# Deferring the evacuation of the energy matmuls behind the next tile's normalization, and a self-wait on every DMA transpose

## The chip, the cores and the metric

The kernel runs on one Trainium2 chip with 8 cores, each running the same program on its own data with no exchange between them. The metric is the device time of the slowest core in microseconds (us); lower is better. PE is the matmul engine (TensorE), DVE the vector engine, ACT the scalar engine, POOL GpSimd, SP the sync engine, which here only issues DMAs.

## The reference, cut to what matters

Input x is 4 batches of 4096 tokens of 1024 numbers. One layer is an attention block and a feed-forward block, each fed by a layernorm and each followed by a layernorm and a residual add.

```python
xn = layernorm(x)                              # stage A
s  = xn @ W_spin.T + b_spin                    # stage A
g  = mean(s, over tokens) @ W_global.T         # stage B
e  = s @ W_J.T                                 # stage A, "energy"
local = softmax(e @ s.T / 32) @ s              # stage C
x1 = x + layernorm(tanh(beta * (s + g + local)))        # stage 2
h  = silu(xn2 @ Wg.T) * (xn2 @ Wu.T)           # stage 3, xn2 = layernorm(x1)
out = x1 + layernorm(h @ Wd.T)                 # stage 4
```

A core takes one half (2048 tokens) of one batch as its own. It needs s for all 4096 tokens of the batch, but e, the attention output and the feed-forward block only for its own 2048.

## The kernel before, in words

The program is written engine by engine with explicit semaphores. Each helper emits its instructions at the end of the queue of the engine that it names, and each engine runs its queue strictly in the order of emission. So the order in which the Python code calls the helpers is the order of work, and an instruction that waits holds back everything behind it on its engine.

**Stage A** walks over 32 tiles of 128 tokens, numbered k. A tile passes through these steps, all of them with two buffers by the parity of k:

- `emit_xchunk(c)`, line 168, SP: loads tiles 2c and 2c+1 of x (1 MB). The load of a chunk waits for `pa_apply` of the odd tile that frees its buffer, and is issued at once after it.
- `pa_stats(k)`, lines 186 to 197: mean and variance on DVE, then the square root on ACT.
- `pa_apply(k)`, lines 210 and 215, DVE: the normalized tile `xn_bf`.
- `pa_xntr(k)`, line 232, a DMA transpose issued from ACT: `xn_bf` into `xnT_sb`.
- `pa_mm(k)`, lines 252 and 256, PE: twice a bias matmul and 8 matmuls of 128x512, into `ps_s`.
- `pa_bias(k)`, line 267, ACT: copies `ps_s` to `s_tok`.
- `pa_stra(k)`, line 277, a DMA transpose issued from ACT: `s_tok` into `s_FM`.

Between these lie the 32 **energy groups**, numbered gi, which exist for the first 16 tiles only. Group gi is 8 matmuls on PE into one of two halves of `ps_e` (line 306), an evacuation on DVE to `e_stage` (line 318), and a write of 128 KB to DRAM issued from POOL (line 327). Eight groups (one `tb`) need four transposed tiles of `s_FM`. The matmuls of group gi wait for the evacuation of group gi-2, and the evacuation of gi waits for the DRAM write of gi-2.

The loop over k emits, in this order: statistics of tile k, normalization and transpose of tile k-1, copy and transpose of s of tile k-2, matmuls of tile k-1, and then as many energy groups as are allowed: the four tiles of s must have been emitted, and gi must be below 2(k-3). A group becomes possible only every fourth k, and so 4, 2, 2 and 0 groups are emitted in turn from k = 5 to k = 20.

The DVE queue between two tiles is thus: statistics of k, normalization of k-1, evacuations of the groups that PE computes after tile k-1, then statistics of k+1, normalization of k, and so on.

**Stage B** (lines 381 to 460) forms the mean and g. **Stage C** takes 16 tiles of 128 queries against 4096 keys in four quarters: scores on PE (line 526), their maximum on DVE (545, 549), the exponential on ACT (570), a DMA transpose issued from ACT (589), a correction by DVE (646), and the second matmul on PE (678). The exponential of a quarter waits for the transpose of the same quarter of the query tile before (line 567), because both use one quarter of `P_sb`. **Stage 2** (lines 803 to 892) forms x1 and its normalized, transposed copy without PE. **Stage 3** (984, 995, 1018) and **stage 4** (1088) are the feed-forward block.

The DMA transposes increment one of four semaphores: `dtp[0]`, `dtp[1]`, `dts[0]`, `dts[1]`. In stage A each takes every second tile; in stage C each belongs to one quarter; in stage 2 `dtp` takes every second tile.

Of the kernel before, what the change touches and what calls it, by code (L numbers as in the profile page):

```python
# [20 lines left out]
KC = D // P  # L21
# [14 lines left out]
def build_program():  # L36
# [19 lines left out]
    with ctx:  # L56
# [20 lines left out]
        def vinc(sem, instr, k=1):  # L77
            instr.then_inc(sem.h, k)
            sem.n += k
            return sem.n  # L80
# [13 lines left out]
        rec = {}  # L94
        sdefer = []

        def s_add(fn):
            sdefer.append(fn)

        def s_flush():  # L100
            fns = list(sdefer)
            del sdefer[:]
            if fns:
                def run(s, fns=fns):
                    for f in fns:
                        f(s)
                block.scalar(run)
# [68 lines left out]
        def pa_stats(k):  # L176
            c, par = k // 2, k % 2
            xsl = xs[:, c % 2, par, :]
            w_sq = rec.get(("sqrt", k - 2), 0)

            def fvA(v, k=k, c=c, par=par, xsl=xsl, w_sq=w_sq):
                w = rec[("xchunk", c)]
                v.wait_ge(w[0].h, w[1])
                if w_sq:
                    v.wait_ge(ss.h, w_sq)
                v.bn_stats(out=st6[:, par, 0:6], in_=xsl[:, 0:512])
                i = v.bn_stats(out=st6[:, par, 6:12], in_=xsl[:, 512:1024])
                vinc(sv, i)
                v.wait_ge(sv.h, sv.n)
                i = v.bn_aggr(out=mvb[:, par, :], in_=st6[:, par, :])  # L190
                vinc(sv, i)
            block.vector(fvA)
            rec[("statsA", k)] = sv.n

            def fsq(s, k=k, par=par, wA=sv.n):
                s.wait_ge(sv.h, wA)
                s.activation(out=sqv[:, par, :], in_=mvb[:, par, 1:2],
                             func=AF.Sqrt, bias=eps_col[:]).then_inc(ss.h, 1)
            s_add(fsq)
            ss.n += 1  # L200
            rec[("sqrt", k)] = ss.n
# [62 lines left out]
        def pa_bias(k):  # L264
            def fsb(s, k=k, par=k % 2, wt=rec[("mm", k)]):
                s.wait_ge(st.h, wt)
                s.copy(out=s_tok[:, k, :], in_=ps_s[:, par, :]).then_inc(ss.h, 1)
            s_add(fsb)
            ss.n += 1
            rec[("biasS", k)] = ss.n  # L270

        def pa_stra(k):
            sem = dts[k % 2]

            def fdt(s, k=k, sem=sem):
                s.wait_ge(ss.h, rec[("biasS", k)])
                s.dma_start_transpose(
                    out=s_FM[:, :, k * P:(k + 1) * P],
                    in_=s_tok[:, k, :]).then_inc(sem.h, 16)
            s_add(fdt)  # L280
            sem.n += 16
            rec[("stra", k)] = (sem, sem.n)
            if k % 4 == 3:
                rec[("stra4", k // 4)] = (dts[0].n, dts[1].n)

        e_sc_w = e_d.rearrange("n p j t -> p n j t")
        eq_groups = [(m, tb) for tb in range(4) for m in range(KC)]
        eg_state = {"i": 0}

        def emit_energy_group():  # L290
            gi = eg_state["i"]
            m, tb = eq_groups[gi]
            eg_state["i"] = gi + 1
            slot = gi % 2
            w_wr = rec.get(("e_wr", gi - 2), 0)

            def fte(t, m=m, tb=tb, slot=slot, gi=gi):
                if gi == 0:
                    t.wait_ge(dwB.h, 16)
                w4 = rec[("stra4", tb)]  # L300
                t.wait_ge(dts[0].h, w4[0])
                t.wait_ge(dts[1].h, w4[1])
                if gi >= 2:
                    t.wait_ge(sv.h, rec[("e_evac", gi - 2)])
                for j in range(KC):
                    i = t.matmul(ps_e[:, slot, :],  # L306
                                 wjT_sb[:, j, m * P:(m + 1) * P],
                                 s_FM[:, j, tb * 512:(tb + 1) * 512],
                                 start=(j == 0), stop=(j == KC - 1))
                vinc(st, i)  # L310
            block.tensor(fte)
            rec[("e_mm", gi)] = st.n

            def fve(v, m=m, tb=tb, slot=slot, gi=gi, w_wr=w_wr):
                v.wait_ge(st.h, rec[("e_mm", gi)])
                if w_wr:
                    v.wait_ge(w_wr[0].h, w_wr[1])
                i = v.tensor_copy(out=e_stage[:, slot, :], in_=ps_e[:, slot, :])  # L318
                vinc(sv, i)
            block.vector(fve)  # L320
            rec[("e_evac", gi)] = sv.n

            sem = deG[gi % 2]

            def fgw(gp, m=m, tb=tb, slot=slot, gi=gi, sem=sem):
                gp.wait_ge(sv.h, rec[("e_evac", gi)])
                gp.dma_start(
                    out=e_sc_w[:, 4 * tb:4 * tb + 4, m, :],
                    in_=e_stage[:, slot, :].rearrange("p (a t) -> p a t", a=4)
                    ).then_inc(sem.h, 16)  # L330
            block.gpsimd(fgw)
            sem.n += 16
            rec[("e_wr", gi)] = (sem, sem.n)
            if (m, tb) == (KC - 1, tb):
                rec[("e_tb", tb)] = (deG[0].n, deG[1].n)

        for k in range(NT_ALL + 2):
            if k < NT_ALL:
                pa_stats(k)
            if 1 <= k < NT_ALL + 1:  # L340
                pa_apply(k - 1)
                pa_xntr(k - 1)
            if 2 <= k:
                pa_bias(k - 2)
                pa_stra(k - 2)
            if 1 <= k < NT_ALL + 1:
                pa_mm(k - 1)
                if (k - 1) % 2 == 1:
                    c2 = (k - 1) // 2 + 2
                    if c2 < NT_ALL // 2:  # L350
                        emit_xchunk(c2)
            while (eg_state["i"] < len(eq_groups)
                   and ("stra", 4 * eq_groups[eg_state["i"]][1] + 3) in rec
                   and eg_state["i"] < max(0, (k - 3)) * 2):
                emit_energy_group()
        while eg_state["i"] < len(eq_groups):
            emit_energy_group()
        s_flush()
        ctxA1.close()
        sv_pa_done = rec[("apply", NT_ALL - 1)]  # L360
# [218 lines left out]
        def c_fptr(qt, qi):  # L579
            par = qt % 2  # L580
            sem = ptx[qi]
            w_pv = rec.get(("pvb", qt - 2, qi), 0)

            def fptr(s, qt=qt, qi=qi, par=par, sem=sem, w_pv=w_pv,
                     wss=rec[("expq", qt, qi)]):
                s.wait_ge(ss.h, wss)
                if w_pv:
                    s.wait_ge(st.h, w_pv)
                s.dma_start_transpose(  # L589
                    out=PT_sb[:, par, qi * 1024:(qi + 1) * 1024]  # L590
                    .rearrange("p (j q) -> p j q", j=8),
                    in_=P_sb[:, qi * 1024:(qi + 1) * 1024]
                    ).then_inc(sem.h, 16)
            s_add(fptr)
            sem.n += 16
            rec[("ptr", qt, qi)] = (sem, sem.n)
# [8 lines left out]
        for qt in range(NT_OWN):  # L605
            par = qt % 2
# [262 lines left out]
        def l2_grpB(t_i):  # L869
            par = t_i % 2  # L870

            def fv2b(v, t_i=t_i, par=par):
                v.wait_ge(ss.h, rec[("sq3", t_i)])
                i = v.reciprocal(out=rsig2[:, par, :], in_=sqv2[:, par, :])
                vinc(sv, i)
                v.wait_ge(sv.h, sv.n)
                if t_i >= 2:
                    w = rec[("xtr", t_i - 2)]
                    v.wait_ge(w[0].h, w[1])
                i = v.tensor_scalar(out=xn2_bf[:, par, :], in0=x1_buf[:, par, :],  # L880
                                    scalar1=mvb2[:, par, 0:1],
                                    scalar2=rsig2[:, par, :],
                                    op0=ALU.subtract, op1=ALU.mult)
                vinc(sv, i)
            block.vector(fv2b)
            rec[("xn2", t_i)] = sv.n

            sem_tr = dtp[t_i % 2]

            def fs3b(s, t_i=t_i, par=par, sem=sem_tr, wv=rec[("xn2", t_i)]):  # L890
                s.wait_ge(sv.h, wv)
                s.dma_start_transpose(
                    out=xn2T[:, :, t_i * P:(t_i + 1) * P],
                    in_=xn2_bf[:, par, :]).then_inc(sem.h, 16)
            s_add(fs3b)
            sem_tr.n += 16
            rec[("xtr", t_i)] = (sem_tr, sem_tr.n)
# [71 lines left out]
        for hb in range(HC):  # L969
            par = hb % 2  # L970
# [106 lines left out]
        for t_i in range(NT_OWN):  # L1077
            par = t_i % 2
# [140 lines left out]
```

## Time and profile before

| | us |
|---|---|
| median of 3 runs (lowest, highest) | 1571.98 (1570.0, 1573.46) |
| profiled execution, its own time | 1574.13 |
| its span on the slowest core, core 7 | 1572.6 |
| spans of the eight cores | 1557.6 to 1572.6 |
| PE busy over the span | 1208.0 (77%) |
| DVE busy | 495.0 (31%) |
| ACT busy | 223.1 (14%) |
| mean DMA rate over the span | 83 GB/s |

All times below are of the profiled execution, on core 7, counted from the start of its span. "Idle before" is the time in which an engine had nothing running ahead of an instruction, with what ended it.

### The profile page before, as it was taken

The page shows a single profiled execution, that of the slowest core. Times are in us where ns is not written, and L with a number is a line of the kernel's source. Part 1 is how long each engine was busy: PE and PEld are TensorE (multiplying, and loading weights), DVE is VectorE, ACT ScalarE, POOL GpSimd, SP SyncE. Part 2 cuts the span into 40 slices and gives each one's busy share as a digit, 9 for nine tenths or more (in the row PEclk, how much of TensorE's full clock was granted, in tenths as well). Part 3 has the DMA queues.
Part 4 walks back from the last instruction along what each step waited for, and adds up shares of the span by engine and source line. Part 5 has one row for each costly group of instructions (what it writes and reads, how often), then busy time and mean ns, then how long its engine had stood idle before and what let it go on. Part 6 is the DMA issues. An engine that isn't in the chain of part 4 may idle for free.

```text
span 1572.6 us, 14760 instructions; the slowest of 8 cores (1557.6 to 1572.6 us)
## 1 busy us (share of the span) xinstructions
PE 1208.0 (77%) x5274; PEld 517.5 (33%) x5274; DVE 495.0 (31%) x860; ACT 223.1 (14%) x359; POOL 72.9 (5%) x92
## 2 busy tenths in 40 slices
PE   0746556568699899989998970009999999999997
PEld 0212122122234344434443430004444444444443
DVE  2221222232124333433343335751222111124334
ACT  0100000011022211211122111001111111110000
POOL 0000011000000000000000000010111111100000
PEclk9977688689889999989999995559999999999999
DMA  9533333285422321222123117976453645503332
GB/s 189 101 91 81 74 80 74 67 189 113 71 50 47 68 48 41 63 52 47 41 50 65 41 27 230 292 141 78 40 71 37 76 46 57 64 28 107 108 107 80
DMA packets 230263, 131.02 MB, mean 83 GB/s; under 512 B 204592, under 2 KB 204592, under 8 KB 230192
## 3 DMA queue, kind: packets, MB, share of 16 engines
q10 hardware_dynamic: 156672, 50.35, 15.8%
q0 software_dynamic: 57744, 29.37, 14.4%
q1 hardware_dynamic: 15776, 50.37, 10.4%
q8 instruction: 43, 0.70, 0.2%
q14 instruction: 28, 0.23, 0.1%
HBM read 92.31 MB, written 25.17 MB: 75 GB/s over the span
## 4 chain that ended last, share of the span: by engine, by line
PE 60%; DMA 13%; DVE 12%; ACT 6%; ACTq 5%; issue 4%; DVEq 0%; SPq 0%; POOL 0%; POOLq 0%
PE ps_pv L678 15%; PE ps_g L984 11%; PE ps_d L1088 11%; PE ps_u L995 11%; PE ps_s L256 8%; DMA xnT_sb<-xn_bf 7%; ACT P_sb L570 4%; ACTq L589 4%; PE ps_e L306 3%; PE ps_s L252 1%; DVE tmp L696 1%; DMA xs<-x 1%; DVE tmp L701 1%; DVE qm L545 1%; ACT attn_wb L714 1%
## 5 line engine op out<-in xcount | busy, mean ns | idle before, releaser
L678 PE MATMUL ps_pv<-s_tok,PT_sb 128*128 128x512 bf16 x1024 | 235.1, 392 | 49.3 <-DVE PT_sb L646 49.3
L984 PE MATMUL ps_g<-xn2T,wg_sb 128*128 128x512 bf16 x768 | 171.6, 382 | 121.1 <-DMA wu_sb<-wuT 121.1
L526 PE MATMUL ps_q<-s_FM,ebuf 128*128 128x512 bf16 x1024 | 226.2, 382 | 4.1 <-DMA ebuf<-e_sc 4.1
L995 PE MATMUL ps_u<-xn2T,wu_sb 128*128 128x512 bf16 x768 | 169.7, 379 | 0.0
L1088 PE MATMUL ps_d<-wdT_sb,h_act 128*128 128x512 bf16 x768 | 165.9, 379 | 1.0 <-DVE h_act L1018 1.0
L678 PEld LDWEIGHTS ps_pv<-s_tok,PT_sb 128*128 128x128 bf16 x1024 | 101.9, 101 | 182.5 <-issue 72.2
L252 PE MATMUL ps_s<-b_row,ones_row 1*128 1x512 bf16 x64 | 29.3, 458 | 168.7 <-DMA xnT_sb<-xn_bf 168.5
L1018 DVE SCALAR_TENSOR_TENSOR h_act<-silu_b,ps_u 128x512 bf16<-128x512 f32 x96 | 66.0, 688 | 283.6 <-PE ps_u L995 283.6
L256 PE MATMUL ps_s<-wspT_sb,xnT_sb 128*128 128x512 bf16 x512 | 149.8, 445 | 0.0
L984 PEld LDWEIGHTS ps_g<-xn2T,wg_sb 128*128 128x128 bf16 x768 | 75.5, 98 | 213.5 <-issue 124.2
L526 PEld LDWEIGHTS ps_q<-s_FM,ebuf 128*128 128x128 bf16 x1024 | 100.8, 98 | 127.2 <-issue 8.1
L1088 PEld LDWEIGHTS ps_d<-wdT_sb,h_act 128*128 128x128 bf16 x768 | 75.1, 98 | 91.9 <-issue 1.5
L995 PEld LDWEIGHTS ps_u<-xn2T,wu_sb 128*128 128x128 bf16 x768 | 75.2, 98 | 90.5
L570 ACT ACTIVATE P_sb<-ps_q,biasq,c_inv 128x1024 bf16<-128x1024 f32 x64 | 77.2, 1207 | 166.3 <-DVE biasq L549 118.2
L1009 ACT ACTIVATE silu_b<-ps_g 128x512 f32<-128x512 f32 x96 | 57.4, 598 | 269.3 <-DVE h_act L1018 154.8
L545 DVE TENSOR_REDUCE qm<-ps_q 128x1 f32<-128x1024 f32 x64 | 78.0, 1219 | 43.2 <-PE ps_q L526 42.8
L318 DVE CAST e_stage<-ps_e 128x512 bf16<-128x512 f32 x32 | 22.1, 692 | 200.7 <-PE ps_e L306 191.3
L696 DVE SCALAR_TENSOR_TENSOR tmp<-ps_pv,rinv,g_bc 128x1024 f32<-128x1024 f32 x16 | 20.5, 1284 | 184.1 <-PE ps_pv L678 184.1
L256 PEld LDWEIGHTS ps_s<-wspT_sb,xnT_sb 128*128 128x128 bf16 x512 | 50.7, 109 | 82.1 <-issue 49.6
L252 PEld LDWEIGHTS ps_s<-b_row,ones_row 1*128 1x128 bf16 x64 | 6.0, 94 | 201.5 <-issue 201.5
L945 POOL DMA_DIRECT2D wg_sb<-wgT x24 | 21.1, 878 | 922.9 <-DMA xn2T<-xn_bf 650.5
L306 PE MATMUL ps_e<-s_FM,wjT_sb 128*128 128x512 bf16 x256 | 57.2, 379 | 0.6 <-DMA s_FM<-s_tok 0.4
(74 smaller groups left out, 526.9 us busy)
## 6 DMA issues: line engine op xcount, KB each, us to landing
xs<-x SPq DMA_DIRECT2D x16, 1024.0 KB, 5.8
xs<-x SPq DMA_DIRECT2D x4, 2048.0 KB, 13.2
x_sc<-x_buf ACTq DMA_DIRECT2D x16, 512.0 KB, 3.9
xs<-x_sc SPq DMA_DIRECT2D x16, 512.0 KB, 4.7
out<-out_b SPq DMA_DIRECT2D x16, 512.0 KB, 5.5
wg_sb<-wgT POOLq DMA_DIRECT2D x24, 256.0 KB, 4.5
wu_sb<-wuT POOLq DMA_DIRECT2D x24, 256.0 KB, 5.4
wdT_sb<-wdT POOLq DMA_DIRECT2D x4, 1536.0 KB, 13.4
```

Of the source, the lines that this page charges most:

```text
L256: i = t.matmul(ps_s[:, par, nb * 512:(nb + 1) * 512], xnT_sb[:, par, j * P:(j + 1) * P], wspT_sb[:, j, nb * 512:(nb + 1) * 512], start=Fal ...
L306: i = t.matmul(ps_e[:, slot, :], wjT_sb[:, j, m * P:(m + 1) * P], s_FM[:, j, tb * 512:(tb + 1) * 512], start=(j == 0), stop=(j == KC - 1))
L526: i = t.matmul(ps_q[:, slot, half * 512:(half + 1) * 512], ebuf[:, qt % 2, j, :], s_FM[:, j, qi * 1024 + half * 512: qi * 1024 + (half + 1 ...
L545: i = v.reduce_max(out=qm4[:, cp, qi:qi + 1], in_=ps_q[:, slot, :], axis=AX.X)
L570: s.activation(out=P_sb[:, qi * 1024:(qi + 1) * 1024], in_=ps_q[:, slot, :], func=AF.Exp, bias=biasq[:, cp, qi:qi + 1], scale=c_inv32[:], ...
L589: s.dma_start_transpose(out=PT_sb[:, par, qi * 1024:(qi + 1) * 1024] .rearrange("p (j q) -> p j q", j=8), in_=P_sb[:, qi * 1024:(qi + 1) * ...
L678: i = t.matmul(ps_pv2[:, nb * 512:(nb + 1) * 512], PT_sb[:, par, cb * P:(cb + 1) * P], s_tok[:, cb, nb * 512:(nb + 1) * 512], start=(cb == ...
L984: i = t.matmul(ps_g[:, tb, :], wg_sb[:, par, j, :], xn2T[:, j, tb * 512:(tb + 1) * 512], start=(j == 0), stop=(j == KC - 1))
L995: i = t.matmul(ps_u[:, tb, :], wu_sb[:, par, j, :], xn2T[:, j, tb * 512:(tb + 1) * 512], start=(j == 0), stop=(j == KC - 1))
L1009: s.activation(out=silu_b[:, tb % 2, :], in_=ps_g[:, tb, :], func=AF.Silu).then_inc(ss.h, 1)
L1018: i = v.scalar_tensor_tensor(out=h_act[:, hb, tb * 512:(tb + 1) * 512], in0=silu_b[:, tb % 2, :], scalar=INV127, in1=ps_u[:, tb, :], op0=A ...
L1088: i = t.matmul(ps_d[:, par, nb * 512:(nb + 1) * 512], h_act[:, cb, t_i * P:(t_i + 1) * P], wdT_sb[:, cb, nb * 512:(nb + 1) * 512], start=( ...
```

## The change

It has three parts.

1. The emission of an energy group is split. `emit_energy_mm` puts its matmuls on PE as before. `emit_energy_evac` (evacuation on DVE, write from POOL) is called one iteration later, after the statistics, the normalization and the transpose of that iteration have been emitted and before its `pa_mm`. The list `pending_evac` carries the groups over.
2. The groups are paced: at most 2 in one iteration, and gi below 2(k-4) in place of 2(k-3). From k = 5 to k = 20 this gives 2 groups in every iteration. The test on `stra4` is the same condition as the one on `stra` that it replaces.
3. Before each DMA transpose of `s_tok` (stage A), `P_sb` (stage C) and `xn2_bf` (stage 2), ACT also waits for the transpose before it on the same semaphore. The transpose of `xn_bf` in stage A is unchanged.

```diff
-            def fdt(s, k=k, sem=sem):
+            def fdt(s, k=k, sem=sem, w_self=sem.n):
                 s.wait_ge(ss.h, rec[("biasS", k)])
+                s.wait_ge(sem.h, w_self)
                 s.dma_start_transpose(
...
-        def emit_energy_group():
-            gi = eg_state["i"]
+        pending_evac = []
+
+        def emit_energy_mm(gi):
             m, tb = eq_groups[gi]
-            eg_state["i"] = gi + 1
             slot = gi % 2
-            w_wr = rec.get(("e_wr", gi - 2), 0)
...
+        def emit_energy_evac(gi):
+            m, tb = eq_groups[gi]
+            slot = gi % 2
+            w_wr = rec.get(("e_wr", gi - 2), 0)
+
             def fve(v, m=m, tb=tb, slot=slot, gi=gi, w_wr=w_wr):
...
             if 2 <= k:
                 pa_bias(k - 2)
                 pa_stra(k - 2)
+            for gi in pending_evac:
+                emit_energy_evac(gi)
+            del pending_evac[:]
             if 1 <= k < NT_ALL + 1:
                 pa_mm(k - 1)
...
             while (eg_state["i"] < len(eq_groups)
-                   and ("stra", 4 * eq_groups[eg_state["i"]][1] + 3) in rec
-                   and eg_state["i"] < max(0, (k - 3)) * 2):
-                emit_energy_group()
+                   and ("stra4", eq_groups[eg_state["i"]][1]) in rec
+                   and len(pending_evac) < 2
+                   and eg_state["i"] < max(0, (k - 4)) * 2):
+                emit_energy_mm(eg_state["i"])
+                pending_evac.append(eg_state["i"])
+                eg_state["i"] += 1
...
             def fptr(s, qt=qt, qi=qi, par=par, sem=sem, w_pv=w_pv,
-                     wss=rec[("expq", qt, qi)]):
+                     wss=rec[("expq", qt, qi)], w_self=sem.n):
                 s.wait_ge(ss.h, wss)
+                s.wait_ge(sem.h, w_self)
                 if w_pv:
...
-            def fs3b(s, t_i=t_i, par=par, sem=sem_tr, wv=rec[("xn2", t_i)]):
+            def fs3b(s, t_i=t_i, par=par, sem=sem_tr, wv=rec[("xn2", t_i)],
+                     w_self=sem_tr.n):
                 s.wait_ge(sv.h, wv)
+                s.wait_ge(sem.h, w_self)
                 s.dma_start_transpose(
```

## Rows read from the trace of the kernel before

**Rows 1.** Stretches of core 7: length, busy time (instructions) by engine, clock, DMA share, GB/s
```profile
66.00:332.00 266.00, 152.63 (x545) 54.90 (x544) 63.45 (x123) 21.25 (x33) 24.05 (x32) 0.76 0.36 84
332.00:399.00 67.00, 51.32 (x202) 18.28 (x202) 19.91 (x42) 14.83 (x21) 0.00 (x0) 0.95 0.65 132
434.00:946.00 512.00, 458.34 (x2048) 202.39 (x2045) 189.40 (x350) 106.11 (x161) 0.00 (x0) 0.97 0.23 48
1062.00:1397.00 335.00, 333.65 (x1536) 150.73 (x1536) 65.82 (x96) 58.72 (x97) 40.98 (x47) 0.99 0.48 55
```

**Rows 2.** Waits, 66 to 332: engine, line, waited for; total us, times, longest
```profile
DVE e_stage L318 <- PE ps_e L306: 191.3, 24, 17.6
...
PE ps_s L252 <- DMA xnT_sb<-xn_bf: 112.8, 12, 10.9
```

**Rows 3.** Timeline, PE: the first energy groups and the last matmuls of tile 20
```profile
65.94 7.07 PE L306 MATMUL ps_e<-s_FM,wjT_sb 128*128 128x512 bf16 x32
...
330.13 1.90 PE L256 MATMUL ps_s<-wspT_sb,xnT_sb 128*128 128x512 bf16 x8
```

**Rows 4.** Timeline, all engines: from one tile to the next, no x load
```profile
222.71 3.62 PE L306 MATMUL ps_e<-s_FM,wjT_sb 128*128 128x512 bf16 x16
...
226.51 0.69 DVE L318 CAST e_stage<-ps_e 128x512 bf16<-128x512 f32 x1 [1.03 <-PE ps_e L306]
227.11 0.68 DVE L186 BATCH_NORM_STATS2 st<-xs 128x6 f32<-128x512 f32 x1
...
228.93 0.81 DVE L215 TENSOR_SCALAR xn_bf<-xs,mvb,rsig 128x1024 bf16<-128x1024 f32 x1 [0.18 <-DVE rsig L210]
229.88 1.23 ACTq L232 DMA_TRANSPOSE xnT_sb<-xn_bf  x1
...
233.22 0.58 PE L252 MATMUL ps_s<-b_row,ones_row 1*128 1x512 bf16 x1 [6.89 <-DMA xnT_sb<-xn_bf]
```

**Rows 5.** Timeline: the same with an x load beside the transpose
```profile
209.94 1.23 ACTq L232 DMA_TRANSPOSE xnT_sb<-xn_bf  x1
...
212.36 3.15 ACTq L277 DMA_TRANSPOSE s_FM<-s_tok  x1
...
216.90 0.58 PE L252 MATMUL ps_s<-b_row,ones_row 1*128 1x512 bf16 x1 [10.78 <-DMA xnT_sb<-xn_bf]
```

**Rows 6.** Timeline, PE: a tile after a long wait, and a tile in full
```profile
166.67 0.58 PE L252 MATMUL ps_s<-b_row,ones_row 1*128 1x512 bf16 x1 [6.85 <-DMA xnT_sb<-xn_bf]
...
173.59 3.62 PE L306 MATMUL ps_e<-s_FM,wjT_sb 128*128 128x512 bf16 x16
...
259.82 0.38 PE L252 MATMUL ps_s<-b_row,ones_row 1*128 1x512 bf16 x1
...
264.36 7.07 PE L306 MATMUL ps_e<-s_FM,wjT_sb 128*128 128x512 bf16 x32 [0.17 <-issue]
```

**Rows 7.** Timeline, PE: the first instruction of a tile after three shorter waits
```profile
51.36 0.37 PE L252 MATMUL ps_s<-b_row,ones_row 1*128 1x512 bf16 x1 [3.07 <-DMA xnT_sb<-xn_bf]
...
353.63 0.58 PE L252 MATMUL ps_s<-b_row,ones_row 1*128 1x512 bf16 x1 [5.08 <-DMA xnT_sb<-xn_bf]
...
365.51 0.37 PE L252 MATMUL ps_s<-b_row,ones_row 1*128 1x512 bf16 x1 [1.70 <-DMA xnT_sb<-xn_bf]
...
368.13 0.60 PE L252 MATMUL ps_s<-b_row,ones_row 1*128 1x512 bf16 x1
```

**Rows 8.** Chain of work that ended last, stretch 343 to 354: start, length, what
```profile
345.00 8.39 DMA xnT_sb<-xn_bf
```

**Rows 9.** Chain of work that ended last, ACT's waits ahead of a transpose in stage C
```profile
571.73 0.02 ACTq L586
571.74 0.04 issue
571.78 0.02 ACTq L588
```

More of the change, by code:

```diff
@@ L333, in emit_energy_group @@
             rec[("e_wr", gi)] = (sem, sem.n)
-            if (m, tb) == (KC - 1, tb):
+            if m == KC - 1:
                 rec[("e_tb", tb)] = (deG[0].n, deG[1].n)
@@ L352, in build_program @@
             while (eg_state["i"] < len(eq_groups)
-                   and ("stra", 4 * eq_groups[eg_state["i"]][1] + 3) in rec
-                   and eg_state["i"] < max(0, (k - 3)) * 2):
-                emit_energy_group()
+                   and ("stra4", eq_groups[eg_state["i"]][1]) in rec
[4 more added lines that the diff above has]
+                eg_state["i"] += 1
+        for gi in pending_evac:
+            emit_energy_evac(gi)
+        del pending_evac[:]
         while eg_state["i"] < len(eq_groups):
-            emit_energy_group()
+            emit_energy_mm(eg_state["i"])
+            emit_energy_evac(eg_state["i"])
+            eg_state["i"] += 1
         s_flush()
```

## The prediction

> **What bounds the kernel now.** I read the page first: PE is busy for 77% of the span, so I looked for the stretches where it is not. The view of stretches gives them [rows 1]. From 434 on, in stages C, 3 and 4, PE is nearly always at work at a granted clock of 0.97 or more (stage 2, between C and 3, has no matmuls, and the change adds only waits there). The stretch 66 to 332, in which stage A computes the energy groups, has PE busy for only 152.6 of 266 us, at a mean granted clock of 0.76. Right behind it, in 332 to 399, the same tiles pass without energy groups, at a clock of 0.95.
>
> The waits of that stretch tell what is missing [rows 2]: PE waits 112.8 us for the transposed tile `xnT_sb`, 12 times for the 16 tiles, and DVE waits 191.3 us for the energy matmuls. 152.6 + 112.8 = 265.4 us, the whole stretch. Its ends in the timeline are the start of the first groups, 65.94, and the end of the matmuls of tile 20, 330.13 + 1.90 = 332.03 [rows 3]: **266.1 us** for 16 tiles and 32 groups.
>
> The timeline shows how the two waits hang together [rows 4]. The two groups of a tile end on PE at 222.71 + 3.62 = 226.33. DVE evacuates the last of them at 226.51, and only then come the statistics of the next tile (227.11), its normalization (228.93) and its transpose (229.88), which lands for PE at 233.22. PE has stood still for 6.89 us, and nothing in this chain needed the energy matmuls: DVE's queue order alone ties the next tile to them. Every second tile has a 1 MB load of x released together with its transpose. There the idle time is 10.78 us: the transpose is issued at 209.94 and PE starts at 216.90 [rows 5].
>
> **Part 1 and 2, the deferred evacuation.** It removes no instruction. In DVE's queue, after tile k's groups on PE, the next normalization now stands ahead of their evacuation. What DVE does behind the evacuation is the statistics and normalization of the tile after the next. So the chain of [rows 4] stays as long as it is, 6.89 or 10.78 us from the end of a tile's groups, but it now releases the matmuls of the tile after the next, and PE has one tile and two groups to do meanwhile.
>
> That cover: a tile at the full clock runs from 259.82 to 264.36 less 0.17 idle, 4.37 us, and two groups take half of 7.07, 3.53 us [rows 6]. Together 7.9 us. It hides the 6.89 us wholly, and the 10.78 us up to 2.9. The other queues fit in: ACT's copy and second transpose of a tile follow the end of that tile's matmuls, 3.53 us before the end of its groups, and the slow issue of 3.15 us [rows 5] then still ends before the square root that comes next, which waits for statistics about 2.4 us after that end. DVE is busy 63.45 us and POOL 24.05 us in the stretch [rows 1], far under the new length. The second evacuation now waits for a write of an iteration ago in place of one in the same burst, and the pace of 2, 2, 2, 2 in place of 4, 2, 2, 0 gives each tile the same cover. What is late next is thus the transpose with the x load beside it.
>
> A pair of tiles then takes 7.9 + 10.78 = 18.7 us, and 8 pairs 149.4 us, with 8 x 2.9 = 23 us of PE idle left.
>
> The clock is the unknown. A tile after a wait of 6.85 us takes 173.59 - 166.67 = 6.92 us in place of 4.37, because its first matmuls run at 1.2 GHz: 2.55 us more [rows 6]. After a wait of 3.07 us the first matmul is at full speed (0.37 us), after 5.08 us it is not (0.58 us), and once the clock fell inside a tile after a wait of only 1.70 us (0.60 us at 368.13) [rows 7]. The new wait of 2.9 us is nearest to the 3.07. I count two of the eight waits as ones after which the clock is low, 5 us; the bounds are 0 and 8 x 2.55 = 20 us. The stretch takes 149.4 + 5.1 = 154.5 us. **Gain 266.1 - 154.5 = 111.6 us.**
>
> The stretch behind it (tiles 21 to 31) keeps its instructions and its order, and so its time; two evacuations more at its start lie in DVE's idle time. The first tiles up to 65.94 are unchanged too.
>
> **Part 3, the self-waits.** A satisfied wait costs ACT 0.02 us and 0.04 us of issue [rows 9]. In stage C three transposes of each query tile lie on the chain that ended last, so 3 x 16 x 0.06 = 2.9 us more. They don't block: the exponential just before has already waited for the same semaphore at the same value. In stage 2, 16 x 0.06 = 1 us at most, and the value was reached before DVE wrote the tile. In stage A the transpose two tiles earlier has long landed (it takes 8.39 us at worst [rows 8], two tiles take 18.7), and ACT has slack: nothing, with 32 x 0.06 = 2 us as the upper bound. Behind such a wait on ACT stands the next square root or exponential. I take **4 us** together; bounds 0 and 6.
>
> **Sum.** 1574.1 - 111.6 + 4 = 1466.5 us for an execution like the profiled one, which lies 2.2 us above the median of the runs. Against that median I predict **1464 us**. The likeliest case's own range, by its clock, is 1459 to 1480.
>
> **Rivals.**
>
> *The DMAs get in each other's way.* In the old stretch they are busy for 0.36 x 266 = 96 us. Packed into 154.5 us that is a share of 0.62, about the 0.65 of 332 to 399 [rows 1], where a transpose of `xn_bf` with the load beside it took 8.39 us [rows 8] against about 6.8 (6.96 less the start of PE) in [rows 5]. That would add 1.6 us to each of the 8 waits, 13 us, and with it the waits grow to 4.5 us, near the 5.08 after which the clock was low: 15 us more. Together 1492. For it speaks that the pace is new; against it, that in the new order the transposes of one tile stand further apart than in 332 to 399. If the even tiles were as slow, the stretch would take 16 x 12.4 = 198 us, and the kernel 1508. The Trainium skill, "DMA: Bandwidth & Descriptors", section "Issuing engines are not separate DMA queues", says that DMAs from all issuing engines run on the same 16 DMA engines and interleave; by that rule the load and the transpose do share their time, and the trace agrees: 10.78 us of idle with the load, 6.89 us without.
>
> *PE alone sets the pace.* If the load no longer met the transpose, the stretch would be 16 x 7.9 = 126.4 us, 28 us less than forecast: 1436. Against it: the load still waits for the same normalization that releases the transpose.
>
> *The self-waits block and take it all back.* If each held ACT until a transpose in flight had landed, it would cost the transpose's 3.3 us (229.88 to 233.22) less the 1.23 us of its issue [rows 4], 2.1 us. Stage C's 48 and stage A's 32 would then cost 168 us, 56 more than the gain: 1572 + 56 = 1628, slower. It decides from 111.6 / 80 = 1.4 us a wait. Against it: the same semaphore has been waited for before, and the other buffers' transposes count on other semaphores.
>
> *The change doesn't loosen PE.* If DVE still came to the normalization late, for instance because an evacuation waits for its write, the time stays, with the 4 us of waits: 1576.
>
> That a busier PE in stage A is granted a lower clock I leave out: in 1062 to 1397 PE works without a pause at 0.99 [rows 1].
>
> **How the numbers follow.** Forecast 0.76; DMAs in the way, 1480 to 1510, 0.12; PE alone, 1430 to 1450, 0.08; self-waits block 0.02; nothing loosened 0.02. The range takes in PE alone and the first step of contention, 1436 to 1492. A measurement of this kernel tells a change from none at about 0.2%, 3 us. Only the last two cases are not faster: slower 0.03, same 0.01, faster 0.96.
>
> **What the profile of the changed kernel would show.** Between the start of the first energy groups and the end of tile 20's matmuls, about 155 us in place of 266. PE's wait for `xnT_sb` in it about 23 us, in about 8 pieces near 3 us, on odd tiles only. The granted clock there well above 0.76, near 0.95. DVE's evacuations right behind a normalization. 332 to 399 of the same length, only earlier, and the query tiles of stage C each about 0.2 us longer. The prediction is wrong if even tiles wait too, if the pieces are over 4 us, or if a transpose waits for its own semaphore.

## The result, and the profile after

| | before | after |
|---|---|---|
| median of 8 runs, us | 1572.11 | 1484.4 |
| lowest, highest | 1568.31, 1575.58 | 1482.86, 1487.39 |
| profiled execution: time, span | 1574.13, 1572.6 | 1484.95, 1483.4 |
| mean of the spans of the 8 cores | 1566.2 | 1473.9 |

The ratio is 0.9448, with a 95% interval of 0.9434 to 0.9461: 88 us faster where 108 were forecast (1464, range 1436 to 1492). All times, ratios and medians here leave out executions in which the cores of one die ran at a visibly lower clock; of one kernel (`c_wait_q0`) a single execution is left, and it was run again as `c_wait_q0b`.

To see where the 20 us are, I took the first and last matmul of each stage from the timelines of all eight cores. The table gives means over the cores.

| stretch, us | before | after | difference |
|---|---|---|---|
| start to first energy group | 67.3 | 68.2 | +0.9 |
| first energy group to tile 31 | 328.6 | 219.2 | -109.4 |
| stage B | 35.2 | 34.2 | -1.0 |
| **stage C** | **503.0** | **521.8** | **+18.8** |
| stage 2 | 122.2 | 120.4 | -1.8 |
| stage 3 | 334.8 | 335.1 | +0.3 |
| sum of these | | | -92.2 |

The sum is the difference of the mean spans. Stage A gave close to what was forecast (109 us less for 112). Stage C took back 19 us where 3 had been set down.

The view of stretches of the changed kernel, slowest core (core 5), has the columns of [rows 1]. Its lines answer to the four there: energy groups, the tiles behind them, stage C, stage 3.

```profile
70.25:223.91 153.66, 132.16 (x544) 51.62 (x544) 59.31 (x114) 20.12 (x32) 24.05 (x32) 0.94 0.57 129
224.00:290.00 66.00, 50.30 (x197) 17.88 (x198) 21.37 (x46) 13.81 (x20) 0.00 (x0) 0.92 0.69 152
325.00:847.00 522.00, 469.31 (x2047) 205.25 (x2048) 186.73 (x347) 104.96 (x160) 0.00 (x0) 0.94 0.23 47
972.90:1308.00 335.10, 334.33 (x1536) 150.79 (x1536) 66.06 (x96) 58.68 (x97) 41.05 (x47) 0.99 0.47 54
```

The first line is the forecast stretch: 153.7 us, for 154.5 forecast and 266.1 before [rows 3]; over the eight cores it took 149.9 to 154.2 us. The granted clock there rose from 0.76 to 0.94. In the third line the clock of stage C is 0.94; it was 0.97 in [rows 1]. Over all eight cores it was 0.97 or 0.98 before and is 0.94 or 0.95 now.

The waits of 70 to 224, changed kernel, which answer to [rows 2] (engine, line, waited for; total us, times, longest):

```profile
DVE e_stage L322 <- PE ps_e L305: 97.4, 32, 10.0
...
PE ps_s L252 <- DMA xnT_sb<-xn_bf: 15.7, 5, 4.5
PE ps_s L252 <- ACT sqv L197: 5.8, 2, 2.9
```

PE's wait for the next tile fell from 112.8 us in 12 pieces to 15.7 + 5.8 = 21.5 us in 7 pieces. (The two put down to ACT are the same kind, with the load beside them; a wait for several semaphores is put down to one.)

The timeline of one odd tile of the changed kernel, which answers to [rows 4, 5]:

```profile
144.49 0.37 SPq L168 DMA_DIRECT2D xs<-x  x1
144.55 1.23 ACTq L232 DMA_TRANSPOSE xnT_sb<-xn_bf  x1
145.14 3.62 PE L305 MATMUL ps_e<-s_FM,wjT_sb 128*128 128x512 bf16 x16
...
147.02 3.60 ACTq L278 DMA_TRANSPOSE s_FM<-s_tok  x1
...
148.93 0.69 DVE L322 CAST e_stage<-ps_e 128x512 bf16<-128x512 f32 x1 [1.03 <-PE ps_e L305]
...
152.01 0.37 PE L252 MATMUL ps_s<-b_row,ones_row 1*128 1x512 bf16 x1 [3.26 <-DMA xnT_sb<-xn_bf]
...
152.32 3.55 PE L256 MATMUL ps_s<-wspT_sb,xnT_sb 128*128 128x512 bf16 x8
...
156.12 1.90 PE L256 MATMUL ps_s<-wspT_sb,xnT_sb 128*128 128x512 bf16 x8
```

The transpose of the next tile is now issued at 144.55, before PE has even started this tile's groups (145.14). In [rows 4] it came 3.55 us after they had ended. PE still waits 3.26 us, because the transpose needs 7.5 us to reach PE (144.55 to 152.01) with the load of x (144.49) beside it. The tile's first matmul, at 152.01, is at full speed (0.37 us), but the eight behind it take 3.55 us where the next eight take 1.90: the clock fell just after the pause had ended.

In stage C, the chain of work around one transpose, changed kernel, which answers to [rows 9]:

```profile
435.69 0.02 issue
435.72 0.02 ACTq L601
435.73 0.04 issue
435.77 0.02 ACTq L602
435.79 0.04 issue
435.83 0.02 ACTq L604
```

Line 602 is the new wait. It is satisfied when ACT comes to it and takes its 0.06 us. The waits of 325 to 847 put PE's pause ahead of the second matmul at 52.6 us in 16 pieces, which were 49.3 us over stage C on the profile's page of the kernel before: 3.3 us more, for 2.9 forecast. But PE's busy time in stage C is longer too, by 11 us on the slowest core (469.3 after; 458.3 in [rows 1]), for the same 2048 matmuls; with the 3.3 us of pause this is the growth of the stage between these two cores, 14.1 us. The timeline shows which:

```profile
441.03 13.97 PE L694 MATMUL ps_pv<-s_tok,PT_sb 128*128 128x512 bf16 x64 [3.32 <-DVE PT_sb L662]
...
471.85 15.66 PE L694 MATMUL ps_pv<-s_tok,PT_sb 128*128 128x512 bf16 x64 [3.03 <-DVE PT_sb L662]
...
504.34 15.40 PE L694 MATMUL ps_pv<-s_tok,PT_sb 128*128 128x512 bf16 x64 [3.02 <-DVE PT_sb L662]
```

Each line is the second matmul of one query tile, 64 instructions, with the pause ahead of it in brackets. It takes 13.97 us at the full clock (2.4 GHz), and 1.3 to 3.0 us more where a part of it runs at 1.2 GHz. It need not begin there. The one at 471.85 starts at the full clock, which falls 1.3 us later (stretches, columns as in [rows 1]; PE has no pause in them):

```profile
471.85:473.00 1.15, 1.15 (x6) 0.56 (x7) 0.89 (x3) 0.00 (x0) 0.00 (x0) 1.00 0.23 46
473.20:476.40 3.20, 3.20 (x9) 1.15 (x8) 1.81 (x6) 0.86 (x1) 0.00 (x0) 0.50 0.00 0
476.70:485.00 8.30, 8.30 (x41) 3.75 (x39) 0.00 (x0) 0.14 (x2) 0.00 (x0) 1.00 0.17 32
```

In the kernel before, 6 of the 16 on the slowest core had such a part; now 13 have. I leave out the last query tile of each core, which has a pause of over 6 us and is slow in both. Of the other 120 on the eight cores, 100 ran wholly at the full clock before, and 31 do now.

### The profile page after: what moved, and what is told of

The parts are those of the page before. It is cut to its first block, busy times and chain, and to the rows that moved or that the text cites. A ratio compares the mean times of both kernels' runs of the same rounds, so it can differ in the third digit from the quotient of the medians.

```text
span 1483.4 us, 14872 instructions; the slowest of 8 cores (1461.2 to 1483.4 us)
## 1 busy us (share of the span) xinstructions
PE 1199.7 (81%) x5274; PEld 516.8 (35%) x5274; DVE 494.9 (33%) x860; ACT 223.0 (15%) x359; POOL 73.0 (5%) x92
## 4 chain that ended last, share of the span: by engine, by line
PE 61%; DMA 12%; DVE 11%; ACT 6%; ACTq 5%; issue 4%; DVEq 0%; SPq 0%; POOL 0%; POOLq 0%
PE ps_pv L694 17%; PE ps_g L1002 11%; PE ps_d L1106 11%; PE ps_u L1013 11%; PE ps_s L256 6%; DMA xnT_sb<-xn_bf 6%; ACT P_sb L585 4%; ACTq L605 4%; PE ps_e L305 3%; DMA xn2T<-xn_bf 2%; DMA xs<-x 1%; DVE tmp L712 1%; DVE tmp L717 1%; DVE qm L560 1%; ACT attn_wb L730 1%
## 5 line engine op out<-in xcount | busy, mean ns | idle before, releaser
L694 PE MATMUL ps_pv<-s_tok,PT_sb 128*128 128x512 bf16 x1024 | 246.2, 405 | 52.6 <-DVE PT_sb L662 52.6
L256 PE MATMUL ps_s<-wspT_sb,xnT_sb 128*128 128x512 bf16 x512 | 134.3, 409 | 0.0
L252 PE MATMUL ps_s<-b_row,ones_row 1*128 1x512 bf16 x64 | 26.3, 411 | 80.3 <-DMA xnT_sb<-xn_bf 74.5
L256 PEld LDWEIGHTS ps_s<-wspT_sb,xnT_sb 128*128 128x128 bf16 x512 | 47.3, 103 | 69.3 <-issue 29.6
L267 ACT CAST s_tok<-ps_s 128x1024 bf16<-128x1024 f32 x32 | 32.4, 1013 | 134.2 <-PE ps_s L256 132.0
```

Source lines behind the costliest of these rows:

```text
L256: i = t.matmul(ps_s[:, par, nb * 512:(nb + 1) * 512], xnT_sb[:, par, j * P:(j + 1) * P], wspT_sb[:, j, nb * 512:(nb + 1) * 512], start=Fal ...
L694: i = t.matmul(ps_pv2[:, nb * 512:(nb + 1) * 512], PT_sb[:, par, cb * P:(cb + 1) * P], s_tok[:, cb, nb * 512:(nb + 1) * 512], start=(cb == ...
```

## The experiments

Theory W: the self-waits lengthen PE's pause, and after the longer pause the clock more often falls. Rival H: the clock falls in stage C because PE was busier in stage A. Each kernel was timed beside the kernel before on the same chip; C is the mean of stage C over the eight cores. Neither theory says which query tiles become slow; that is taken up behind `c_wait_x4`.

**c_wait_out.** The changed kernel, without the self-wait in stage C:

```diff
                 s.wait_ge(ss.h, wss)
-                s.wait_ge(sem.h, w_self)
                 if w_pv:
```

> The changed kernel without the self-wait in stage C (stages A and 2 keep theirs). Theory W: the three extra waits per query tile lengthen PE's pause ahead of the second matmul from 2.85 to 3.05 us, and after the longer pause the clock falls; stage C returns from 522 to about 503 us and the kernel from 1484 to about 1466. Theory H: the clock falls in stage C because stage A now keeps PE busier beforehand, and the waits cost only their 3 us; stage C 519, the kernel 1481.

Measured: 1462.66 us beside 1567.58, ratio 0.9338 (0.9302 to 0.9374); C 501.0 us. Two of its query tiles, with the pauses in brackets:

```profile
439.39 13.97 PE L693 MATMUL ps_pv<-s_tok,PT_sb 128*128 128x512 bf16 x64 [3.14 <-DVE PT_sb L661]
470.03 13.97 PE L693 MATMUL ps_pv<-s_tok,PT_sb 128*128 128x512 bf16 x64 [2.85 <-DVE PT_sb L661]
```

The pause is 2.85 us again (0.3 us longer at about every fourth query tile), 108 of the 120 second matmuls run at the full clock, and 20.8 us of stage C are gone. Stage A is as busy as in the changed kernel (219.0 us), so H falls.

**c_wait_alone.** The kernel before, with the self-wait in stage C alone:

```diff
                 s.wait_ge(ss.h, wss)
+                s.wait_ge(sem.h, w_self)
                 if w_pv:
```

> The kernel before with the self-wait in stage C alone. Theory W: stage C grows from 503 to about 522 us, the kernel from 1572 to about 1590, at a lower clock in the tiles whose pause exceeds 3 us. Theory H: 3 us more, 1575, the clock in stage C as before.

Measured: 1585.4 us, ratio 1.0113 (1.0089 to 1.0136); C 520.3 us. That is 17.3 us more than before, with stage A left as it was (326.6 us). The self-waits in stage C cost this from either side, whatever stage A does.

**c_wait_q0b.** The kernel before, with four self-waits at the first quarter's transpose only, which ACT issues while PE is at the second matmul:

```diff
                 s.wait_ge(ss.h, wss)
+                if qi == 0:
+                    s.wait_ge(sem.h, w_self)
+                    s.wait_ge(sem.h, w_self)
+                    s.wait_ge(sem.h, w_self)
+                    s.wait_ge(sem.h, w_self)
                 if w_pv:
```

The first run, c_wait_q0:

> The kernel before with four self-waits per query tile, all of them at the first quarter's transpose in stage C, which is issued while PE works through the second matmul. Theory W (what counts is the length of PE's pause): the pause stays 2.85 us, the clock and stage C too, and the kernel stays at 1568 to 1572. If it is the number of wait instructions on ACT that costs, it is 1585 or more.

And the second:

> The same kernel as c_wait_q0 once more, whose times were nearly all disturbed. As there: 1568 to 1576 if the length of PE's pause is what counts, since these waits lie beside the second matmul; 1585 or more if the number of wait instructions on ACT is.

Measured in the second: 1573.7 us beside 1570.2, ratio 1.0021 (1.0002 to 1.0040). The first rests on one execution, 1575.83 us, with C 505.2 us. Four more instructions per query tile, where the change adds four as well, cost 2 to 4 us when they lie beside PE's work, and 17 when three of them lie in its pause. The place counts, not the number.

**c_wait_x4.** The kernel before, with four self-waits ahead of every transpose of stage C:

```diff
                 s.wait_ge(ss.h, wss)
+                for _ in range(4):
+                    s.wait_ge(sem.h, w_self)
                 if w_pv:
```

> The kernel before with four self-waits ahead of each transpose in stage C. Each adds 0.06 us to each of three transposes, so the pause grows from 2.85 to about 3.55 us. Theory W: every query tile now has a low clock behind its pause: 16 x 0.7 = 11 us of pause and 16 x about 2 us of clock, less what the kernel before already had, so stage C 503 + 11 + about 25 = 540 us and the kernel about 1605. Were the pause harmless, 1580.

Measured: 1606.4 us, ratio 1.0226 (1.0204 to 1.0248); C 538.9 us, as worked out. The pauses are 3.5 us and more, but not every query tile is slow: 23 of 120 run at the full clock. The stretch of stage C on core 5, columns as in [rows 1], shows PE busy for 475.7 us at a clock of 0.92:

```profile
431.00:970.00 539.00, 475.71 (x2038) 205.91 (x2036) 187.88 (x348) 104.65 (x160) 0.00 (x0) 0.92 0.22 46
```

So a longer pause in all query tiles goes with more slow ones. The length of the single pause doesn't decide, though. In `c_wait_out`, 30 of 32 pauses of 3.1 to 3.3 us have the full clock behind them; in the changed kernel, only 17 of 63 pauses between 2.9 and 3.1 us do. And a slow query tile is mostly followed by a slow one. I counted the fourth to the fifteenth query tile on all cores of the changed kernel: 72 of the 76 that follow a slow one are slow, and 9 of the 20 that follow a fast one. In `c_wait_out` these are 2 of 4 and 2 of 92. A longer pause also makes the query tile longer: 471.85 - 441.03 = 30.82 us in the changed kernel where the clock holds, 470.03 - 439.39 = 30.64 us in `c_wait_out`. No run here separates the pause's length from the moment at which it falls, so what makes a given query tile slow stays open.

**x_load_late.** The changed kernel, with the load of x released one step later:

```diff
                 if w_ss:
                     sync.wait_ge(sv.h, w_ss)
+                    sync.wait_ge(w_xt[0].h, w_xt[1])
```

where `w_xt` is the landing of the odd tile's transpose, `rec[("xntr", 2c-3)]`.

> The changed kernel, with the load of the next two tiles of x released by the landing of the odd tile's transpose in place of its normalization. If the load beside the transpose is what leaves PE waiting on every second tile in the stretch of the energy groups (8 waits of about 3 us, and the slow clock after some of them), the stretch falls from 154 to about 128 us and the kernel from 1484 to about 1458. If the transposes are slow because all DMAs are denser now, the waits stay: 1480 to 1490.

Measured: 1451.5 us, ratio 0.9257 (0.9236 to 0.9278). The first energy group to tile 31 takes 192.9 us in place of 219.2. The stretch of the energy groups on its slowest core:

```profile
67.70:193.70 126.00, 124.27 (x544) 50.27 (x544) 60.55 (x117) 21.09 (x33) 24.05 (x32) 1.00 0.69 167
```

PE is busy for 124.3 of 126 us at a clock of 1.00, and its waits in that stretch hold no wait for `xnT_sb` (four other cores have one or two short waits ahead of a tile, at most 2.4 us together). The DMAs are denser than in the changed kernel (0.69 for 0.57), and it does no harm. So the waits left over came from the one load beside the one transpose. The general contention of the first rival is not what makes them.

**pace_alone.** The kernel before with the pacing but not the deferral:

```diff
+            n_it = 0
             while (eg_state["i"] < len(eq_groups)
+                   and n_it < 2
                    and ("stra", 4 * eq_groups[eg_state["i"]][1] + 3) in rec
-                   and eg_state["i"] < max(0, (k - 3)) * 2):
+                   and eg_state["i"] < max(0, (k - 4)) * 2):
                 emit_energy_group()
+                n_it += 1
```

> The kernel before with the pacing of 2 groups in each iteration alone, the evacuation not deferred and no self-waits. If the deferral is what lifts the wait, each of the 16 tiles now shows its pause of 6.9 or 10.8 us, where before one in four was hidden: the stretch grows from 266 to about 305 us, the kernel to about 1610. If the even pace does part of the gain by itself, the kernel becomes faster than 1572.

Measured: 1605.75 us, ratio 1.0239 (1.0220 to 1.0257). Its waits, 65 to 369:

```profile
PE ps_s L252 <- DMA xnT_sb<-xn_bf: 138.9, 17, 10.5
```

Every tile has its pause now, 138.9 us for 112.8 in [rows 2]. The pacing is a loss by itself; with the deferral it gives each tile the same cover. The deferral without the pacing wasn't tried: groups of one iteration wait for the evacuation two groups earlier, which the deferral emits only in the next iteration.

**ahead_only and best.** PE's pause in stage C can be filled. `ahead_only` is the changed kernel, self-waits kept, with the scores of the second quarter of the next query tile ahead of the second matmul:

```diff
             if qt + 1 < NT_OWN:
                 c_scq(qt + 1, 0)
+                c_scq(qt + 1, 1)
```

> The changed kernel, self-waits kept, with PE computing the scores of the second quarter of the next query tile (3.45 us) too ahead of the second matmul, in place of behind it. The pause of 3.05 us is filled. If the pause and the clock behind it are the whole loss, stage C falls from 522 to about 16 x 27.8 + 25 = 470 us and the kernel from 1484 to about 1432. Rival: the pause only moves to the scores, since the exponentials on ACT come no earlier: 1475 to 1484.

Measured: 1462.46 us, ratio 0.9308 (0.9293 to 0.9322); C 504.1 us. Neither expectation held as written. A query tile on core 4:

```profile
463.41 7.07 PE L541 MATMUL ps_q<-s_FM,ebuf 128*128 128x512 bf16 x32 [1.85 <-ACT P_sb L585]
471.54 13.97 PE L696 MATMUL ps_pv<-s_tok,PT_sb 128*128 128x512 bf16 x64 [1.06 <-DVE PT_sb L664]
```

The pause is not filled but split, 1.85 + 1.06 us, so the query tile keeps its 30.8 us. But the clock no longer falls: on every core all second matmuls but the last take 13.8 to 14 us, and 17.7 us of stage C come back although the self-waits are still there. So neither the self-waits nor the longer query tile costs the clock by itself; it takes the pause in one piece.

`best` joins this, the later load and the self-wait's removal in stage C.

> The changed kernel without the self-wait in stage C, with the load of x released by the transpose, and with the scores of the second quarter ahead of the second matmul. If the three gains add, 1484 - 32 (load) - 52 (scores ahead, which makes the self-wait's removal worth about nothing more) = 1400; if filling the pause fails as in the rival of the run before, about 1430.

Measured: 1430.3 us, ratio 0.9108 (0.9092 to 0.9123); C 500.4 us: the second value, since the pause was only split. Both this kernel and `ahead_only` keep the full clock behind all pauses but the last, so their difference in stage C, 3.7 us, is the cost of the self-waits without the clock.

**exp1_early.** `best`, with maximum, exponential and transpose of that second quarter moved too:

```diff
             if qt + 1 < NT_OWN:
                 c_fvq(qt + 1, 0)
+                c_fvq(qt + 1, 1)
...
                 c_fexp(qt + 1, 0)
                 c_fptr(qt + 1, 0)
+                c_fexp(qt + 1, 1)
+                c_fptr(qt + 1, 1)
```

> The kernel of the run best with, further, the maximum, the exponential and the transpose of the second quarter of the next query tile emitted right behind those of its first, ahead of the tanh of the tile at hand. In the run best PE's pause was only split (0.85 us ahead of the second matmul, 1.85 us ahead of the third quarter's scores), the cycle stayed 30.6 us. If the cycle is set by three exponentials with their transposes in a row on ACT behind the tanh, two in a row take 2.8 us less: a cycle of 27.8 to 28 us, stage C 500 - 15 x 2.7 = 460 us, the kernel about 1390. If something else holds the cycle, 1430.

Measured: 1387.34 us, ratio 0.8836 (0.8812 to 0.8859); C 456.6 us. The timeline of PE on the slowest core:

```profile
431.33 13.97 PE L699 MATMUL ps_pv<-s_tok,PT_sb 128*128 128x512 bf16 x64
445.14 13.98 PE L543 MATMUL ps_q<-s_FM,ebuf 128*128 128x512 bf16 x64
459.14 13.97 PE L699 MATMUL ps_pv<-s_tok,PT_sb 128*128 128x512 bf16 x64
```

And the stretch of stage C, columns as in [rows 1]:

```profile
300.00:740.00 440.00, 432.45 (x1984) 193.57 (x1983) 185.90 (x347) 104.74 (x160) 0.00 (x0) 0.99 0.26 56
```

From one second matmul to the next are 459.14 - 431.33 = 27.8 us, without a pause; PE is busy for 98% of the stretch. What had held the query tile at 30.6 us was the chain that ends in ACT's three exponentials with their transposes in a row behind the tanh; with two in a row it is no longer the limit. This version is 97 us faster than the changed kernel.

## Why the prediction was right, and where it was off

- **The deferral (right).** The chain from a tile's groups to a tile's matmuls kept its length and now spans one tile more. The stretch took 153.7 us for 154.5. `pace_alone` shows that the pacing by itself gives nothing; the deferral was run only together with it. That 153.7 comes so near to 154.5 is in part luck: PE's work at the full clock was 124.3 us for 126.4 and its pauses 21.5 for 23, and the slow clock took 3 us more than counted.
- **What is left (right, with one exception).** Pauses of 2.6 to 4.5 us, 21.5 us in all for 23, on odd tiles only, seven of them: tile 5 had none. The one of 4.5 us is over the 4 us that were to be a sign against the prediction; the other six are 2.6 to 3.3 us. `x_load_late` took them away by moving the load, as the step that blames the load says.
- **The slow clock in stage A (too small, inside its bounds).** 2 of 8 waits at 2.55 us had been counted, 5 us. PE was busy for 132.2 us in the stretch and for 124.3 in `x_load_late` at clock 1.00, so it cost 8 us: the clock was low behind four of the seven waits, at about 2 us each. The prediction had read the clock behind a wait from the first matmul alone [rows 7]; at 152.01 that one is fast, and the clock falls behind it.
- **"PE alone sets the pace".** Not the changed kernel, but `x_load_late` is this rival: 126 us for the 126.4 worked out, and 1451.5 us for the kernel where 1436 had been worked out, because its stage C still has the slow clock.
- **The self-waits (the term that was mis-sized).** "I take 4 us together; bounds 0 and 6." Their own time was right, 0.06 us each. But the term measured 20.8 us in stage C by taking the waits out, and 17.3 us by putting them into the kernel before. (Stage C without them takes 501.0 us in one kernel and 503.0 in the other.) The prediction priced a longer pause at its length alone. For stage A it had asked what the clock does after a pause of 2.9 us [rows 7]; for stage C, where PE's pause stood at the same length and 16 tiles depend on it, it did not ask. Put in place of the 4 us, they make 1464 into 1477 to 1481, where 1484 was measured. The last 3 to 7 us are not traced to the change: the slowest core after has a start and a stage 2 each 4.4 us longer than the slowest core before, and both differ by as much between the cores of one kernel.
- **A busier stage A and a lower clock.** Left out of the sum with reason: `c_wait_out` has the busy stage A and the old stage C.
- **The self-waits block.** They do not; no new wait for them shows in stage C.

## What to carry to other kernels

An engine queue that is strictly in order ties unrelated work together: if the evacuation of side work stands ahead of the main chain's next step, emit it one iteration later, and pace the side work so that every iteration has the same cover. When a few hundredths of a microsecond are added to a chain, ask whether PE stands in a pause at its end, once in every turn of a loop. Here pauses a little longer cost the clock for 1.3 to 3.0 us behind many of them, and splitting the pause gave that back although its sum stayed. Release a large load behind a small urgent transfer, not beside it.

## What the runs showed of the hardware

- PE's pause ahead of the second matmul in stage C, the stage's mean over the cores, and the clock of its stretch on one core: usual pause 2.85 us, 503.0 us, 0.97; 3.05 us, 521.8 us, 0.94; 3.5 us, 538.9 us, 0.92; a pause split into 1.85 and 1.06 us, 504.1 us, full speed behind all but the last pause. The second matmuls wholly at the full clock, of 120 on all cores, are 100, 31, 23 and 120. The step from the first to the second is 0.2 us a tile, 3 us in all. In the same kernel, pauses of one length have either clock behind them. Where a tile was slow in the changed kernel, 53 of 89 began at 1.2 GHz and 36 at 2.4 GHz, the clock falling a little later. The Trainium skill, "TensorE: Matmul & The Clock Gate", section "HAM oscillation — how this bites in real kernels", describes bursts of matmuls with waits for DMA between them, each burst beginning at the slow clock. This trace agrees in part: with pauses near 3 us, which end here with DVE's work, most bursts lose the clock, but not each one, and many lose it only after they have begun.
- A satisfied semaphore wait costs ACT 0.06 us: 3 x 0.06 x 16 = 2.9 us, measured as 3.3 us of pause, and as 3.7 us of stage C between `ahead_only` and `best`.
- Some pauses are 0.3 us longer (3.14 in place of 2.85 in `c_wait_out`, about one in four; 3.32 in place of 3.02 in the changed kernel, about two in five), at other query tiles in each kernel. What causes it stays open.
